# Flamingo cross-attention with experts on one core: the first two pairs' key/value work moved ahead of x's transposes

## The chip, the cores and the metric

The kernel runs on one core of a Trainium2 chip. The metric is the time of one execution in device microseconds (us). Engines are named as in the profile: PE is TensorE (PEld its weight loads), DVE is VectorE, ACT is ScalarE, POOL is GpSimd, SP is SyncE, which here only issues DMAs. A trailing q (SPq, ACTq) marks an engine's sequencer, which issues transfers.

## The reference, cut to what matters

There are 16 batches of 56 rows of x with 256 features, and for each batch 1500 context rows with 256 features. A mask marks padding at the end of each batch's context.

```python
x = x + tanh(g_xattn) * xattn(layernorm(x), ctx, mask, Wq, bq, Wk, bk, Wv, bv, Wo, bo, gamma, beta, rs)
x = x + tanh(g_ffn) * ffn(layernorm(x), router_gate, gate_up, down)   # 8 experts, top 2
...
q = clean(hs @ Wq.T + bq); k = clean(at @ Wk.T + bk); v = clean(at @ Wv.T + bv)   # 16 heads of 16
scores = clip(where(mask > 0.5, clip(q @ k.T / 4, -50, 50), -10000), -50, 50)
probs = softmax(scores); ctx = probs @ v
delta = layernorm(clip(rs, 0, 0.3) * (ctx @ Wo.T + bo)) * gamma + beta
```

A masked position gets a score of -50, not nothing, so every context row counts in the sums. The kernel adds those with plain sums over the whole context and does keys, values and scores only for tiles of 125 context rows that have a key to attend to.

## The kernel before, in words

**Tiles and pairs.** The context is cut into 12 tiles of 125 rows per batch. Two tiles are worked together as a pair: `k_proj` (L538) makes the pair's keys in one PSUM bank, ACT copies them out with the bias `bk` (`k_copy`, L893), `v_proj` (L545) makes the values in another bank, DVE copies them out with the bias `bv` (`v_copy`, L1134), `scores` (L555) multiplies keys by queries, ACT takes the exponentials (`exps`, L901), DVE clips them (`clips`, L1143), `p_v` (L566) multiplies by the values, and DVE adds the result to `acc` (L1156). `first_kv(n)` is `k_proj` and `v_proj` for pair n of the first four. There is one key bank and one value bank, so a key product waits for ACT's copy of the one before, and a value product for DVE's.

**Two stretches.** The last tile of every batch is in every case worked ("sure" tiles). The first four pairs (flow `first`, batches 0 to 7) are sure tiles and need no list; they fill the time in which x is normalised, the queries are made, and the mask is turned into a list of active tiles (`ranks`, L707 and L708; `lists`, L717 to L724). The list then steers the main pairs: a part of them stands in branches on the number of tiles (`early_pairs`), the rest follows in a row. After them come the experts: 32 steps with `gate_up` (L808) and `down` (L823).

**x's way.** x arrives in two halves (SP, L254 and L257). For each, DVE takes the statistics (L1092, L1098), POOL gives a first guess of the inverse root (L382), DVE refines it (`offsets`, up to L1104), ACT normalises eight tiles of 112 rows (`normalise_rows`, L920), DVE cleans each of them in two steps (`clean_rows`, L1111 and L1112), PE transposes them two at a time (`x_transposes(c)`, L523), ACT copies the transposed rows out (`x_rows`, L865), PE makes queries (`x_queries`, L530), ACT adds `bq` (`query_bias`, L877), DVE cleans them in six steps (`clean_queries`, L1123 to L1129), and ACT spreads them by head (`spread_queries`, L886). `x_transposes(c)` waits for the cleaned tiles 2c and 2c + 1.

**The order** on each engine is written out by hand. Each engine runs its own list, waits on semaphores, and never passes a waiting instruction. SP's queue and ACT's queue issue the transfers in the order of the code. Where the stretch with the first pairs ends, SP fetches the whole context of batch after batch in transfers of 1.5 MB (`fetch_all`, L284) for the plain sums (ACT L913, DVE L1173); each such buffer is fetched again only after its sums are taken.

Of the kernel before, what the change touches and what calls it, by code (L numbers as in the profile page):

```python
# [15 lines left out]
P = 128  # L16
# [11 lines left out]
RPH = PAIRS // 2  # L28
# [41 lines left out]
def flamingo(nc, x_d, ctx_d, mask_d, gx_d, gf_d, wq_d, bq_d, wk_d, bk_d, wv_d, bv_d, bv_col_d, wo_d, bo_d,  # L70
             gamma_d, beta_d, rs_d, router_d, gate_up_d, down_d, out_d):
    with ExitStack() as ctx:
# [94 lines left out]
        x_in = [sem(f"x_in{h}") for h in range(2)]  # L167
        bias_in, small_in, late_in, experts_in = (sem(n) for n in ("bias_in", "small_in", "late_in", "experts_in"))
        pair_in = [sem(f"pair_in{n}") for n in range(RING)]
        all_in = [sem(f"all_in{n}") for n in range(STREAMS)]  # L170
# [75 lines left out]
        def _(sp):  # L246
# [3 lines left out]
            def fetch_sure(n, tile, semaphore):  # L250
                for t in range(2):
                    sp.dma_start(tile[:, t], sure_rows[2 * n + t, :, NT - 1]).then_inc(semaphore, 16)

            sp.dma_start(x_sb[:, 0:RPH], x_rows[:, 0:RPH]).then_inc(x_in[0], 16)  # L254
            fetch_sure(0, ctx_pair[0], first_in[0])
            sp.dma_start(mask_i[:], mask_d.rearrange("(h n) t -> n h t", h=2)).then_inc(mask_in, 16)
            sp.dma_start(x_sb[:, RPH:PAIRS], x_rows[:, RPH:PAIRS]).then_inc(x_in[1], 16)  # L257
            for n in range(1, SURE):
                fetch_sure(n, ctx_pair[n], first_in[n])
# [259 lines left out]
        def _(pe):  # L519
# [76 lines left out]
            def first_kv(n):  # L596
                pe.wait_ge(first_in[n], 32)
                after(pe, first.k_out, n)
                k_proj(ctx_pair[n], first.k_mm)
                if n == 0:  # L600
                    ranks()
                    pe.wait_ge(wv_in, 16)
                after(pe, first.v_out, n)
                v_proj(ctx_pair[n], first.v_mm)
# [136 lines left out]

            pe.wait_ge(wk_in, 16)
            first_kv(0)
            pe.wait_ge(consts, CONSTS_IDENT)
            x_transposes(0)
# [4 lines left out]
            lists()  # L750
            first_kv(1)
            first_scores(0)
# [110 lines left out]
        def _(act_e):  # L863
# [84 lines left out]

            act_e.dma_start(wk[:], wk_d).then_inc(wk_in, 16)
            act_e.dma_start(wv[:], wv_d).then_inc(wv_in, 16)  # L950
            act_e.dma_start(wq[:], wq_d).then_inc(wq_in, 16)
            for tile, source in ((bq, bq_d), (bk, bk_d), (bv_col, bv_col_d)):
                act_e.dma_start(tile[:], source).then_inc(bias_in, 16)
            act_e.dma_start(bv[:], bv_d.partition_broadcast(P)).then_inc(bias_in, 16)
            act_e.wait_ge(spare_clear, 1)
# [5 lines left out]
            def first_exps(n):  # L961
                act_e.wait_ge(mask_ready, 1)
                exps(first, p[n % 2], sure_slots(n), n + 1)

            act_e.wait_ge(x_offset, 1)
            for t in range(RPH):
                normalise_rows(t, x_normal)
            act_e.wait_ge(bias_in, 64)
            first_copy(0)
            x_rows(0)  # L970
            x_rows(1)
            query_bias(0)
            act_e.wait_ge(x_offset, 2)
# [6 lines left out]
            spread_queries(0)  # L980
            first_copy(1)
            first_exps(0)
# [78 lines left out]
        def _(dve):  # L1061
# [281 lines left out]
            moments_of(range(RPH, PAIRS))  # L1343
            for t in range(RPH):
                clean_rows(t)
# [16 lines left out]
                                    ALU.add).then_inc(head_ready, 1)  # L1362
            dve.wait_ge(bias_in, 64)
            v_copy(first, v[0], 1)
            clean_queries(0)
# [8 lines left out]
            clean_queries(1)  # L1374
            v_copy(first, v[1], 2)
            clean_rows(4)
# [12 lines left out]
            first_sums(1)  # L1389
            clean_queries(3)  # L1390
            clips(first, p[1], 7)
            first_sums(2)
            dve.wait_ge(small_in, 48)
# [159 lines left out]
```

## Time and profile before

| what | value |
|---|---|
| median of 3 runs | 266.04 us (265.19 to 266.28) |
| the profiled execution's own time | 265.4 us |
| its span, first to last instruction | 263.7 us |
| PE busy | 226.5 us, 86% of the span |
| DVE busy | 180.2 us, 68% |
| ACT busy | 146.3 us, 55% |
| mean granted TensorE clock | 0.939 of full speed |

Times in the rows below are counted from the span's start. The chain is the work that ended last, followed back from the last instruction; "issue" in it is time in which the engine waited for nothing that the profile shows. A granted clock of 1.00 is 2.4 GHz, 0.50 is 1.2 GHz; in the stretch before the first record of the clock the view repeats that first record's value.

### The profile page before, as it was taken

The page shows a single profiled execution, that of the slowest core. Times are in us where ns is not written, and L with a number is a line of the kernel's source. Part 1 is how long each engine was busy: PE and PEld are TensorE (multiplying, and loading weights), DVE is VectorE, ACT ScalarE, POOL GpSimd, SP SyncE. Part 2 cuts the span into 40 slices and gives each one's busy share as a digit, 9 for nine tenths or more (in the row PEclk, how much of TensorE's full clock was granted, in tenths as well). Part 3 has the DMA queues.
Part 4 walks back from the last instruction along what each step waited for, and adds up shares of the span by engine and source line. Part 5 has one row for each costly group of instructions (what it writes and reads, how often), then busy time and mean ns, then how long its engine had stood idle before and what let it go on. Part 6 is the DMA issues. An engine that isn't in the chain of part 4 may idle for free.

```text
span 263.7 us, 7332 instructions
## 1 busy us (share of the span) xinstructions
PE 226.5 (86%) x2820; PEld 195.4 (74%) x2820; DVE 180.2 (68%) x458; ACT 146.3 (55%) x242; POOL 55.8 (21%) x90
## 2 busy tenths in 40 slices
PE   0889897218999999999999979968999489999994
PEld 0777786206888888988888868956899379899993
DVE  1888639710555899865968878687298866865754
ACT  2855679931445779879858781434453136525110
POOL 2470000200143442110002201164114523300000
PEclk9999999556999999999999988999899959999998
DMA  6999304580682289996997000120010000100101
GB/s 218 308 424 413 116 9 114 171 344 2 209 348 60 65 317 340 365 409 191 320 420 301 2 4 2 28 48 0 0 37 1 0 0 2 35 1 0 39 0 35
DMA packets 12871, 37.58 MB, mean 143 GB/s; under 512 B 2320, under 2 KB 10016, under 8 KB 10528
## 3 DMA queue, kind: packets, MB, share of 16 engines
q1 hardware_dynamic: 11728, 36.13, 38.4%
q10 hardware_dynamic: 1008, 0.92, 1.4%
q8 instruction: 25, 0.41, 0.6%
q14 instruction: 14, 0.11, 0.2%
q0 software_dynamic: 96, 0.00, 0.0%
HBM read 35.14 MB, written 0.92 MB: 137 GB/s over the span
## 4 chain that ended last, share of the span: by engine, by line
PE 59%; DVE 17%; issue 12%; ACT 4%; DMA 3%; POOL 3%; SPq 1%; DVEq 0%; ACTq 0%; POOLq 0%
PE bank L808 12%; PE bank L538 11%; PE bank L545 10%; PE bank L566 6%; PE bank L823 6%; PE bank L555 6%; DMA x_sb<-x_dram 3%; POOL guess L382 2%; PE bank L530 2%; PE bank L700 1%; PE bank L523 1%; DVE half_var L1084 1%; DVE stats L1092 1%; DVE acc L1156 1%; DVE normed L1112 1%
## 5 line engine op out<-in xcount | busy, mean ns | idle before, releaser
L808 PE MATMUL bank<-rowsT,gate_up 128*128 128x224 f32 x256 | 58.7, 377 | 0.0
L538 PE MATMUL bank<-ctx_pair,wk 128*128 128x250 f32 x152 | 40.7, 411 | 17.3 <-issue 9.8
L901 ACT ACTIVATE p<-bank,mask_bias,mask_scale 125x896 f32<-125x896 f32 x38 | 39.7, 1095 | 26.7 <-PE bank L555 26.7
L808 PEld LDWEIGHTS bank<-rowsT,gate_up 128*128 128x128 f32 x256 | 51.4, 204 | 2.5 <-issue 0.3
L538 PEld LDWEIGHTS bank<-ctx_pair,wk 128*128 128x128 f32 x152 | 29.2, 202 | 22.9 <-issue 18.0
L545 PE MATMUL bank<-wv,ctx_pair 128*125 128x256 f32 x152 | 37.1, 388 | 0.0
L1021 ACT ACTIVATE silu<-bank 128x224 f32<-128x224 f32 x32 | 11.4, 357 | 46.2 <-PE bank L808 46.2
L1143 DVE TENSOR_SCALAR p<-p 125x912 f32<-125x912 f32 x38 | 27.5, 739 | 11.1 <-ACT p L901 11.1
L823 PE MATMUL bank<-down,act 128*112 128x256 f32 x128 | 33.5, 388 | 0.3 <-DVE act L1443 0.3
L545 PEld LDWEIGHTS bank<-wv,ctx_pair 128*125 128x125 f32 x152 | 29.4, 194 | 4.6
L913 ACT ACTIVATE ctx_all<-ctx_all 128x1500 f32<-128x1500 f32 x19 | 27.9, 1474 | 0.0
L453 POOL COPY q_slot<-qbd 128x224 f32 x22 | 10.9, 496 | 78.6 <-PE bank L555 44.3
L823 PEld LDWEIGHTS bank<-down,act 128*112 128x112 f32 x128 | 23.2, 182 | 4.0 <-DVE act L1443 0.7
L566 PEld LDWEIGHTS bank<-p,v 125*17 125x17 f32 x1344 | 18.2, 99 | 9.1 <-issue 8.4
L382 POOL TENSOR_TENSOR guess<-var_eps,minus_half 112x2 f32<-112x2 f32 (+1 forms) x10 | 9.4, 940 | 72.3 <-DVE var_eps L1077 72.3
L566 PE MATMUL bank<-p,v 125*17 125x57 f32 x1344 | 21.7, 218 | 3.5 <-DVE acc L1156 3.5
L515 POOL TENSOR_TENSOR x_sb<-x_sb,p 112x512 f32<-112x512 f32 x16 | 20.6, 1287 | 18.5 <-ACT p L1029 17.9
L1443 DVE TENSOR_TENSOR act<-silu,bank 128x224 f32<-128x224 f32 x32 | 12.3, 383 | 17.8 <-ACT silu L1021 17.7
L1134 DVE TENSOR_TENSOR v<-bank,bv 125x512 f32<-125x512 f32 x19 | 13.0, 684 | 16.6 <-PE bank L545 16.5
L1156 DVE TENSOR_TENSOR acc<-bank,acc 128x228 f32 (+1 forms) x42 | 16.1, 392 | 9.7 <-DVE acc L1156 4.8
L1029 ACT ACTIVATE p<-bank,weight 112x256 f32<-112x256 f32 x32 | 13.4, 470 | 7.8 <-PE bank L823 5.9
L523 PE MATMUL bank<-ident,normed 112*128 112x112 f32 x32 | 5.1, 285 | 11.1 <-ACT normed L920 7.5
(158 smaller groups left out, 298.4 us busy)
## 6 DMA issues: line engine op xcount, KB each, us to landing
ctx_all<-ctx_dram SPq DMA_DIRECT2D x13, 1500.0 KB, 8.0
ctx_pair<-ctx_dram SPq DMA_DIRECT2D x38, 125.0 KB, 5.2
gate_up<-ctx_dram SPq DMA_DIRECT2D x3, 1500.0 KB, 11.0
gate_up<-gate_up_dram SPq DMA_DIRECT2D x1, 2048.0 KB, 12.8
down<-down_dram SPq DMA_DIRECT2D x1, 1024.0 KB, 14.8
num<-acc SPq DMA_DIRECT2D x16, 57.0 KB
x_sb<-x_dram SPq DMA_DIRECT2D x2, 448.0 KB, 6.1
out_dram<-x_sb SPq DMA_DIRECT2D x4, 224.0 KB, 2.3
```

Of the source, the lines that this page charges most:

```text
L382: nc.gpsimd.tensor_tensor(guess[:, 0:w], var_eps[:, 0:w], minus_half[:, 0:w], ALU.pow).then_inc(guess_out, 1)
L515: nc.gpsimd.tensor_tensor(x_sb[:, rows], x_sb[:, rows], scaled[:, s % 3], ALU.add).then_inc(d_added, 1)
L538: mm = nc.tensor.matmul(bank[:, K_BANK, 2 * TT * m:2 * TT * (m + 1)], wk[:, k, P * m:P * (m + 1)], tile[:, :, k, :], start=(k == 0), stop= ...
L545: mm = nc.tensor.matmul(bank[0:TT, V_BANK, H * t:H * (t + 1)], tile[:, t, k, :], wv[:, k, :], start=(k == 0), stop=(k == HALVES - 1))
L555: mm = nc.tensor.matmul(bank[0:TT, j, DEN * t + R2 * m:DEN * t + R2 * (m + 1)], k_tile[rows, m, TT * t:TT * (t + 1)], q_tiles[t][rows, m]. ...
L566: mm = nc.tensor.matmul(bank[2 * HD * j:2 * HD * j + HD + 1, PV_BANK, ACC * t + SP1 * slot:ACC * t + SP1 * (slot + 1)], v_tile[:, t, v_of( ...
L808: mm = nc.tensor.matmul(bank[:, GU_BANK[s], CHUNK * g:CHUNK * (g + 1)], gate_up[:, e, k, g, :], rowsT[:, k, CHUNK * c:CHUNK * (c + 1)], st ...
L823: mm = nc.tensor.matmul(bank[0:R2, D_BANK[s % 3], H * t:H * (t + 1)], act[:, s % 4, R2 * t:R2 * (t + 1)], down[:, e, :], start=True, stop= ...
L901: nc.scalar.activation(p_tile[:, t].rearrange("t (j n) s -> t j n s", j=4)[:, :, :, 0:S], bank[0:TT, 0:4, DEN * t:DEN * (t + 1)].rearrange ...
L913: nc.scalar.activation(mine, mine, ACT.Identity, accum_out=total[:, k, b:b + 1]).then_inc(act_sum, 1)
L1143: nc.vector.tensor_scalar(tile, tile, E_HI, E_LO, ALU.min, ALU.max).then_inc(flow.p_out, 1)
L1156: nc.vector.tensor_tensor(mine, bank[:, PV_BANK, ACC * t:ACC * (t + 1)].rearrange("p (r s) -> p r s", r=SLOTS), mine, ALU.add).then_inc(fl ...
```

## The change

SP fetches the two tiles of pair 0 ahead of x's first half, and those of pair 1 ahead of the mask and x's second half. ACT's queue fetches `bk` right behind `wk`, with a semaphore of its own, then `wv`, `bv`, `bq`, `bv_col`, and `wq` last instead of third. PE takes keys and values of pair 0, `ranks`, and keys and values of pair 1, and only then x's transposes; before, `ranks` stood inside pair 0 and pair 1 behind `lists`. ACT copies pair 0's keys ahead of normalising x's first half and pair 1's right behind it. DVE copies pair 0's values between the first and the second cleaned tile of x, and pair 1's where pair 0's stood; behind the second `clean_queries` none is left. At the end of the first pairs DVE adds pair 2's sums before it clips pair 3's exponentials, not behind it.

```diff
--- before.py
+++ after.py
@@ -166,6 +166,7 @@
         mask_in, wq_in, wk_in, wv_in = (sem(n) for n in ("mask_in", "wq_in", "wk_in", "wv_in"))
         x_in = [sem(f"x_in{h}") for h in range(2)]
         bias_in, small_in, late_in, experts_in = (sem(n) for n in ("bias_in", "small_in", "late_in", "experts_in"))
+        bk_in = sem("bk_in")
         pair_in = [sem(f"pair_in{n}") for n in range(RING)]
         all_in = [sem(f"all_in{n}") for n in range(STREAMS)]
         pair_in_g = sem("pair_in_g")
@@ -251,11 +252,12 @@
                 for t in range(2):
                     sp.dma_start(tile[:, t], sure_rows[2 * n + t, :, NT - 1]).then_inc(semaphore, 16)
 
+            fetch_sure(0, ctx_pair[0], first_in[0])
             sp.dma_start(x_sb[:, 0:RPH], x_rows[:, 0:RPH]).then_inc(x_in[0], 16)
-            fetch_sure(0, ctx_pair[0], first_in[0])
+            fetch_sure(1, ctx_pair[1], first_in[1])
             sp.dma_start(mask_i[:], mask_d.rearrange("(h n) t -> n h t", h=2)).then_inc(mask_in, 16)
             sp.dma_start(x_sb[:, RPH:PAIRS], x_rows[:, RPH:PAIRS]).then_inc(x_in[1], 16)
-            for n in range(1, SURE):
+            for n in range(2, SURE):
                 fetch_sure(n, ctx_pair[n], first_in[n])
             ctx_rows = ctx_d.rearrange("b p (n f) -> (b p n) f", n=NT)
 
@@ -598,7 +600,6 @@
                 after(pe, first.k_out, n)
                 k_proj(ctx_pair[n], first.k_mm)
                 if n == 0:
-                    ranks()
                     pe.wait_ge(wv_in, 16)
                 after(pe, first.v_out, n)
                 v_proj(ctx_pair[n], first.v_mm)
@@ -741,6 +742,8 @@
 
             pe.wait_ge(wk_in, 16)
             first_kv(0)
+            ranks()
+            first_kv(1)
             pe.wait_ge(consts, CONSTS_IDENT)
             x_transposes(0)
             x_transposes(1)
@@ -748,7 +751,6 @@
             x_queries(0)
             x_queries(1)
             lists()
-            first_kv(1)
             first_scores(0)
             x_transposes(2)
             first_kv(2)
@@ -947,11 +949,12 @@
                                misc(0, 2 * CHUNK).rearrange("p (k n) -> p k n", k=HALVES)).then_inc(misc_out, 1)
 
             act_e.dma_start(wk[:], wk_d).then_inc(wk_in, 16)
+            act_e.dma_start(bk[:], bk_d).then_inc(bk_in, 16)
             act_e.dma_start(wv[:], wv_d).then_inc(wv_in, 16)
+            act_e.dma_start(bv[:], bv_d.partition_broadcast(P)).then_inc(bias_in, 16)
+            for tile, source in ((bq, bq_d), (bv_col, bv_col_d)):
+                act_e.dma_start(tile[:], source).then_inc(bias_in, 16)
             act_e.dma_start(wq[:], wq_d).then_inc(wq_in, 16)
-            for tile, source in ((bq, bq_d), (bk, bk_d), (bv_col, bv_col_d)):
-                act_e.dma_start(tile[:], source).then_inc(bias_in, 16)
-            act_e.dma_start(bv[:], bv_d.partition_broadcast(P)).then_inc(bias_in, 16)
             act_e.wait_ge(spare_clear, 1)
             flat = acc[:].rearrange("p r b s -> p (r b s)")
             nc.scalar.copy(flat, spare[:, 1:2].broadcast_to(flat.shape)).then_inc(zeros_out, 1)
@@ -962,13 +965,15 @@
                 act_e.wait_ge(mask_ready, 1)
                 exps(first, p[n % 2], sure_slots(n), n + 1)
 
+            act_e.wait_ge(bk_in, 16)
+            first_copy(0)
             act_e.wait_ge(x_offset, 1)
             for t in range(RPH):
                 normalise_rows(t, x_normal)
-            act_e.wait_ge(bias_in, 64)
-            first_copy(0)
+            first_copy(1)
             x_rows(0)
             x_rows(1)
+            act_e.wait_ge(bias_in, 48)
             query_bias(0)
             act_e.wait_ge(x_offset, 2)
             for t in range(RPH, RPH + 2):
@@ -978,7 +983,6 @@
                 normalise_rows(t, x_normal)
             act_e.wait_ge(head_ready, 1)
             spread_queries(0)
-            first_copy(1)
             first_exps(0)
             spread_queries(1)
             x_rows(2)
@@ -1341,7 +1345,10 @@
             dve.wait_ge(x_in[1], 16)
             stats_of(range(RPH, PAIRS))
             moments_of(range(RPH, PAIRS))
-            for t in range(RPH):
+            clean_rows(0)
+            dve.wait_ge(bias_in, 48)
+            v_copy(first, v[0], 1)
+            for t in range(1, RPH):
                 clean_rows(t)
             dve.wait_ge(misc_mm, USE["rank"] + 1)
             nc.vector.tensor_copy(rank[:], misc(0, 4, HT)).then_inc(misc_out, 1)
@@ -1360,8 +1367,7 @@
             dve.wait_ge(consts, CONSTS_HEADS)
             nc.vector.tensor_reduce(head_mask[:], head_of[:].rearrange("p (j a) -> p a j", a=2), AX_X,
                                     ALU.add).then_inc(head_ready, 1)
-            dve.wait_ge(bias_in, 64)
-            v_copy(first, v[0], 1)
+            v_copy(first, v[1], 2)
             clean_queries(0)
             dve.wait_ge(misc_mm, USE["list"] + 1)
             nc.vector.tensor_copy(slot_list[:].rearrange("o n s -> o (n s)"), misc(0, 2 * TILES, 1)
@@ -1372,7 +1378,6 @@
             step(nc.vector.tensor_scalar(mask_bias[0:TT], flat_mask, 1.0, CLIP, ALU.subtract, ALU.mult))
             nc.vector.memset(bank[:, PV_BANK, :], 0.0).then_inc(mask_ready, 1)
             clean_queries(1)
-            v_copy(first, v[1], 2)
             clean_rows(4)
             clean_rows(5)
             dve.wait_ge(fill_out, 2 + VRING)
@@ -1388,8 +1393,8 @@
             clips(first, p[0], 5)
             first_sums(1)
             clean_queries(3)
+            first_sums(2)
             clips(first, p[1], 7)
-            first_sums(2)
             dve.wait_ge(small_in, 48)
             step(nc.vector.tensor_scalar(rscale[:], gates[:, 2:3], 0.0, 0.3, ALU.max, ALU.min))
             nc.vector.tensor_scalar(lim[:, 0:1], rscale[0:R2], LIM, None, ALU.mult)
```

PE's list from its first matmul to the third transposes. L538 and L545 are a pair's keys and values, L707 and L708 `ranks`, L523 transposes, L530 queries, L717 to L724 `lists`, L555 scores. Before:

```order
L538 MATMUL bank<-ctx_pair,wk 128x250 x4
L707 MATMUL bank<-active,tri 96x2
L708 MATMUL bank<-active,ones 96x2
L545 MATMUL bank<-wv,ctx_pair 125x256 x4
L523 MATMUL bank<-ident,normed 128x112 x8
L530 MATMUL bank<-rowsT,wq 128x224 x8
L717 MATMUL bank<-pick,vals 1x176 x4
L721 MATMUL bank<-last,attend 125x8 x2
L724 MATMUL bank<-pick,attend 125x176 x2
L538 MATMUL bank<-ctx_pair,wk 128x250 x4
L545 MATMUL bank<-wv,ctx_pair 125x256 x4
L555 MATMUL bank<-qbd,k_sb 125x112 x16
```

The same stretch with the change (its lines stand one or two further on):

```order
L540 MATMUL bank<-ctx_pair,wk 128x250 x4
L547 MATMUL bank<-wv,ctx_pair 125x256 x4
L708 MATMUL bank<-active,tri 96x2
L709 MATMUL bank<-active,ones 96x2
L540 MATMUL bank<-ctx_pair,wk 128x250 x4
L547 MATMUL bank<-wv,ctx_pair 125x256 x4
L525 MATMUL bank<-ident,normed 128x112 x8
L532 MATMUL bank<-rowsT,wq 128x224 x8
L718 MATMUL bank<-pick,vals 1x176 x4
L722 MATMUL bank<-last,attend 125x8 x2
L725 MATMUL bank<-pick,attend 125x176 x2
L557 MATMUL bank<-qbd,k_sb 125x112 x16
```

Pair 1's keys and values went from behind the lists to ahead of the transposes; behind the lists only the scores of pair 0 are left, and then the third transposes.

DVE's list from the variances of x's second half to the copy of `rank`, with the change; before, the same rows stood there without the one of L1138, which is the copy of pair 0's values:

```order
L1115 TENSOR_SCALAR positive<-normed 112x256
L1116 SCALAR_TENSOR_TENSOR normed<-normed,positive 112x256
L1138 TENSOR_TENSOR v<-bank,bv 125x32x16
L1115 TENSOR_SCALAR positive<-normed 112x256
L1116 SCALAR_TENSOR_TENSOR normed<-normed,positive 112x256
```

The copy entered between the first and the second of the four cleaned tiles that the first transposes need.

DVE's list from the clearing of the bank behind the mask's factors to the fifth cleaned tile, before:

```order
L1373 MEMSET bank 128x512
L1123 TENSOR_SCALAR q_clean<-q_raw 128x448
L1124 TENSOR_SCALAR fix_neg<-q_raw 128x448
L1125 TENSOR_SCALAR finite<-q_raw 128x448
L1127 TENSOR_TENSOR q_clean<-q_clean,fix_neg 128x448
L1073 COPY spare<-spare 128x1
L1129 COPY_PREDICATED q_clean<-finite,q_raw 128x448
L1134 TENSOR_TENSOR v<-bank,bv 125x32x16
L1111 TENSOR_SCALAR positive<-normed 112x256
L1112 SCALAR_TENSOR_TENSOR normed<-normed,positive 112x256
```

With the change the same rows stand there but the one of L1134: the copy of pair 1's values left this place.

## Rows read from the trace of the kernel before

**Rows 1.** Chain that ended last: start us, us, what; first transposes to third.

```profile
2.76 7.21 DMA x_sb<-x_dram
...
15.35 0.60 PE bank L523 x4
...
25.01 0.57 issue
...
27.24 0.60 PE bank L523 x4
```

**Rows 2.** Chain that ended last, from the fourth pair to the main pairs.

```profile
46.34 1.06 DVE p L1143 x2
47.40 0.62 DVE acc L1156 x2
...
48.26 1.72 PE bank L566 x64
49.98 7.55 issue
...
58.29 2.26 issue
```

**Rows 3.** Timeline, first 10 us: start, us, engine line op xcount, [idle before <-releaser].

```profile
0.85 0.39 SPq L254 DMA_DIRECT2D x_sb<-x_dram  x1
...
1.29 0.95 SPq L252 DMA_DIRECT2D ctx_pair<-ctx_dram  x2
...
5.76 1.41 DVE L1092 BATCH_NORM_STATS2 stats<-x_sb 112x6 f32<-112x256 f32 x4 [4.38 <-DMA x_sb<-x_dram]
...
7.47 3.67 PE L538 MATMUL bank<-ctx_pair,wk 128*128 128x250 f32 x8 [7.47 <-DMA ctx_pair<-ctx_dram]
...
9.72 0.16 DVE L1104 SCALAR_TENSOR_TENSOR offset<-moments,rstd 112x4 f32<-112x4 f32 x1
```

**Rows 4.** DMA queues, 5 to 6 us: packets, MB, share (q1 SP's, q10 ACT's).

```profile
q10 hardware_dynamic: 136, 0.25, 75.3%
q1 hardware_dynamic: 113, 0.10, 31.2%
```

**Rows 5.** Timeline, 17 to 26 us.

```profile
17.42 0.67 DVE L1134 TENSOR_TENSOR v<-bank,bv 125x512 f32<-125x512 f32 x1
...
20.67 0.84 PE L724 MATMUL bank<-pick,attend 96*125 96x176 f32 x4
20.82 1.23 ACT L886 ACTIVATE qbd<-q_clean,head_mask 128x448 f32<-128x448 f32 x2
...
21.35 1.86 PE L538 MATMUL bank<-ctx_pair,wk 128*128 128x250 f32 x8
...
23.05 1.89 PE L545 MATMUL bank<-wv,ctx_pair 128*125 128x256 f32 x8
...
24.87 1.14 PE L555 MATMUL bank<-qbd,k_sb 32*125 32x112 f32 x32
```

**Rows 6.** Windows: stretch, us, busy of PE, PEld, DVE, ACT, POOL; clock, DMA share, GB/s.

```profile
45.10:47.10 2.00, 0.00 (x0) 0.00 (x0) 1.97 (x5) 1.62 (x3) 0.00 (x0) 1.00 0.46 126
48.20:50.00 1.80, 1.72 (x64) 1.51 (x64) 0.19 (x3) 1.80 (x3) 0.37 (x1) 0.50 0.13 41
60.50:64.20 3.70, 3.65 (x9) 2.97 (x9) 0.00 (x0) 0.54 (x2) 0.00 (x0) 0.50 0.02 4
64.30:66.00 1.70, 1.70 (x35) 1.25 (x37) 0.25 (x1) 0.19 (x1) 0.00 (x0) 1.00 0.00 0
211.70:214.70 3.00, 3.00 (x10) 2.82 (x11) 2.77 (x8) 1.35 (x4) 0.00 (x0) 0.50 0.00 0
214.70:217.80 3.10, 3.10 (x11) 2.50 (x10) 1.76 (x8) 0.72 (x2) 1.94 (x2) 0.50 0.00 0
```

**Rows 7.** Timeline at 49 us: SP's first 1.5 MB fetch behind the first pairs.

```profile
49.23 0.34 SPq L284 DMA_DIRECT2D ctx_all<-ctx_dram  x1
```

**Rows 8.** DMA queues, 54 to 58 us: packets, MB, share of 16 engines.

```profile
q8 instruction: 1, 0.02, 1.4%
```

## The prediction, made before the run

> **What bounds the kernel now.** I read the page first, then the chain of waits, which shows where the start of the kernel is decided; then the timeline of the first 50 us, the windows for the granted clock, and the DMA queues. Up to 60 us the chain is not one engine's: it runs x's transfer, DVE's statistics and cleaning, PE's transposes, queries and lists, DVE's query cleaning, DVE's cleaning of the fifth and sixth tile of x, PE's third transposes [rows 1]. From 27.24 us on PE is packed until the scores of pair 2. Behind the first pairs the chain goes through DVE's clips and sums, PE's last product, and two stretches of 7.55 and 2.26 us in which PE waits for nothing that the profile shows [rows 2]. After that the main pairs run on PE back to back, so what the start loses or gains is passed on to the end.
>
> So the change must be judged by when two things start: the second transposes (15.35 us) and the third (27.24 us) [rows 1]. Both wait for DVE, not for PE.
>
> **The change part by part.**
>
> *Transfers.* x's first half is issued first now, and DVE begins on it at 5.76 us; pair 0's tiles come behind it and release PE at 7.47 us [rows 3]. The change swaps the two. Together they are the same bytes, so x's first half should land at the latest when the tiles did: at most 7.47 - 5.76 = +1.7 us. At least it is issued later by the two issues ahead of it, +0.95 us [rows 3]. Between 5 and 6 us ACT's queue took 75.3% and SP's 31.2% of the DMA engines [rows 4], and with `wq` now last on ACT's queue SP's share there grows a little. I take +1.3. The offsets end at 9.72 + 0.16 = 9.88 us [rows 3] and DVE went on with x's second half at 9.97 (2.76 + 7.21, [rows 1]), so 0.1 of slack is used up: **+1.2 us** (0.8 to 1.7). The second half also has pair 1's tiles ahead of it, again 250 KB, and moves by about as much; DVE reaches it only when the offsets are done, so this isn't added.
>
> The row on the two queues shows them served together. The Trainium skill ("DMA: Bandwidth & Descriptors", section "Queues, rings and completion order") says that each DMA engine takes turns between the queues that have work, and takes one queue's descriptors in order. By that rule x can't pass the tiles on SP's queue, and the delay would be near the upper end; the trace agrees on the sharing, and no row shows the order being broken.
>
> *PE's keys and values ahead of the transposes.* Pair 0 starts with the tiles' landing, before 7.47 us. Its keys took 3.67 us, twice the 1.86 us of pair 1's [rows 3, 5], since TensorE was still at its low clock. Keys and values of both pairs and the ranks fit before the transposes, which DVE releases at about 17 us; only pair 1's values wait, for DVE's copy of pair 0's. I cost this at nothing; the cover is DVE's cleaning, and if PE is still cold at pair 1's values they take 1.7 us more and some 0.9 would show.
>
> *ACT's copies of keys.* Pair 0's now stands ahead of the normalising of x's first half, so all of x waits behind it if the keys or `bk` are late. Even with the old start the keys are done at 7.47 + 3.67 = 11.1 us [rows 3], and the offsets now come at 9.88 + 1.3 = 11.2: nothing, and at most a fraction of a us if the tiles don't land earlier. Pair 1's copy falls where ACT waits for the first transposes: nothing.
>
> *DVE's copy of pair 0's values* now stands between cleaned tiles 1 and 2: 0.67 us [rows 5], on the chain: **+0.7 us**. Before it lay at 17.42 us where DVE waited for the queries; pair 1's copy now has that place and costs nothing there. The second transposes start at about 15.35 + 1.9 = 17.25 us, and queries, lists and the mask's factors shift by as much.
>
> *DVE's copy of pair 1's values* leaves the place behind the second `clean_queries`, where the chain has it as 0.57 us of "issue" at 25.01 [rows 1]: **-0.6 us**. So the third transposes start at 27.24 + 1.2 + 0.7 - 0.6 = 28.5 us.
>
> *The place that pair 1 left on PE.* Before, 1.86 and 1.89 us of keys and values stood between the lists (end 21.51) and the scores of pair 0 at 24.87 [rows 5]. They were not on the chain: DVE's 5.7 us from the lists to the third transposes were. Taking them away brings the scores to the end of the spread queries, 20.82 + 1.23 + 1.9 = 23.95 us, and gains nothing for the third transposes. PE then has 1.14 us of scores in the 5.1 us from 23.4 to 28.5, with the last 3.4 us, from 25.1, idle.
>
> What such a gap does to the clock the trace shows once: PE did its last product of pair 2 by 45.0 us, had nothing to do until 48.26, and the granted clock, still 1.00 (2.4 GHz) to 47.10, was 0.50 (1.2 GHz) when it came back [rows 2, 6]. The low clock then stays for a time after work is back: 3.7 us from 60.50 until it was 1.00 at 64.30, and 6.1 us from 211.70 to 217.80 [rows 6]. Work there takes twice as long, so half of the stretch is lost: 1.85 to 3.05 us. Behind the third transposes PE is packed with keys, values, scores and queries of the chain, so the loss is all on it. The restart is like the one at 60.50 (keys and values without a break), so I take a value near the lower end: **+2.2 us**.
>
> The Trainium skill ("TensorE: Matmul & The Clock Gate", section "Why this matters for your kernels") asks for no long idle gaps between bursts of matmuls, because TensorE falls back to its cold clock. It speaks against this change, and by it the gap costs what I have put in; without it the sum would be that of the first rival. The trace agrees at 48.26 us.
>
> *Sums before clips.* Before: two clips 1.06, sums 0.62, then the product of pair 3, 1.72 [rows 2]. The product needs the sums and for its first half one clip; its second half needs the second clip. With the order turned its first half starts 0.5 us earlier, and it ends 0.5 us earlier. But behind it PE waits 7.55 us, and that stretch ends when code packets come through among the transfers that SP issued at 49.23 [rows 2, 7, 8]. Those hang on ACT's sums, which this edit doesn't move. Between -0.5 and 0, I take **-0.3 us**.
>
> **Sum:** 1.2 + 0.7 - 0.6 + 2.2 - 0.3 = +3.2 us. On the profiled execution (265.4 us) that gives 268.6; it lies 0.6 below the median shown, so against 266.04 the forecast is **269.2 us**. With the bounds of x's delay (0.8 to 1.7), the clock (1.85 to 3.05) and the last edit it runs from +2.3 to +4.9, less if x's delay is overrated.
>
> **The rivals.**
>
> *The clock doesn't fall.* The gap of 3.4 us is about as long as the one that let it fall (3.26), and the scores stand just before it as pair 2's product did there. Against: nothing else in the rows. If it doesn't, or rises at once, the sum is +1.0: 267.0 us. Within half a per cent.
>
> *Faster: code arrives before the transfers.* Of PE's two waits at the branches the first took 7.55 us and the second 2.26 [rows 2]. Between 54 and 58 us a single instruction packet came [rows 8], in a stretch full of the 1.5 MB fetches. The last edit brings PE 0.5 us ahead of ACT's sums, and so of SP's issue at 49.23 [rows 7]. If PE's request then gets ahead of them, the first wait becomes like the second: -5.3 us, the sum 3.2 - 5.3 = -2.1, **263.9 us**. It decides from the point where PE asks before the fetch is in the queues; PE reached the wait at 49.98, 0.75 behind the issue, and 0.5 is short of that. I hold it unlikely but not excluded.
>
> *x isn't late.* If the DMA engines make room for both and x lands as before, the sum is +2.0: 268.0 us. The 0.95 us of issues ahead of it speak against it.
>
> **How the numbers follow.** The forecast has 0.65, the steady clock 0.17, early code 0.13, x on time 0.05. The range of 8 in 10 reaches from 266.4 to 271.4: it takes in the forecast's bounds and the steady clock, and leaves out early code (0.13) and some 0.07 above. A measurement of this kernel can tell about 0.5%, or 1.3 us, from no change: faster 0.13, within 0.5% 0.17 (the steady clock), slower 0.70 (forecast and x on time).
>
> **What would show it.** In the changed profile: DVE's first statistics start near 7 us instead of 5.76, PE's first keys before 7.47; the second transposes near 17.2; an idle gap of more than 3 us ahead of the third transposes, near 28.5; a granted clock of 0.50 behind it, and keys of pair 2 at 3 us or more; the long wait at the branches still there, later by about 3 us. I am wrong if the third transposes start before 27.5 us, if the clock is 1.00 through the gap, or if the wait behind pair 3 shrinks to a few us.

## The result, and the profile after

| | before | changed |
|---|---|---|
| median | 265.62 us (4 runs, 263.01 to 266.28) | 270.68 us (4 runs, 270.14 to 270.99) |
| profiled execution | 265.4 us | 270.92 us |
| its span | 263.7 us | 269.2 us |

The ratio is 1.0207, 95% interval 1.0135 to 1.028: about 5 us slower. The forecast was 269.2 us (range 266.4 to 271.4), slower with 0.70. Ratios, here and below, leave disturbed runs out, so they can lie off the quotient of two medians (e10's rests on three of its ten runs, and the profiled executions of e7 and e10 are disturbed ones). The kernel before was run again beside the experiments; its medians there are 265.4 to 265.7 us, and what is said below to be faster or slower is counted from them.

Chain of waits of the changed kernel (start us, us, what), answering to [rows 1, 2]:

```profile
3.77 9.32 DMA x_sb<-x_dram
...
16.45 2.66 PE bank L547 x8
19.11 1.49 PE bank L525 x8
...
31.63 1.01 PE bank L525 x4
32.64 2.78 PE bank L540 x8
...
52.80 0.55 DVE p L1147
...
53.49 1.05 PE bank L568 x64
54.54 9.25 issue
...
64.54 1.65 issue
66.19 2.92 PE bank L540 x7
```

Three things are new in it. x's second half lands 9.32 us after its issue (7.21 before), at 13.09 instead of 9.97. PE's values of pair 1 (L547 at 16.45) stand on the chain. Keys of pair 2 take 2.78 us, where in the chain of the kernel before they took 1.71.

Timeline of the changed kernel (start, us, engine line op, [idle before <-releaser]), answering to [rows 3, 5]:

```profile
4.93 3.67 PE L540 MATMUL bank<-ctx_pair,wk 128*128 128x250 f32 x8 [4.93 <-DMA ctx_pair<-ctx_dram]
...
7.74 1.40 DVE L1096 BATCH_NORM_STATS2 stats<-x_sb 112x6 f32<-112x256 f32 x4 [6.35 <-DMA x_sb<-x_dram]
...
11.00 0.29 DVE L1340 TENSOR_SCALAR attend<-mask_i 96x250 f32<-96x250 int32 x1 [1.12 <-DMA mask_i<-mask_dram]
...
12.47 1.94 PE L540 MATMUL bank<-ctx_pair,wk 128*128 128x250 f32 x8
...
13.12 1.40 DVE L1096 BATCH_NORM_STATS2 stats<-x_sb 112x6 f32<-112x256 f32 x4 [0.40 <-DMA x_sb<-x_dram]
...
15.71 0.68 DVE L1138 TENSOR_TENSOR v<-bank,bv 125x512 f32<-125x512 f32 x1
...
16.45 2.66 PE L547 MATMUL bank<-wv,ctx_pair 128*125 128x256 f32 x8 [2.04 <-DVE v L1138]
```

Pair 0 starts at 4.93 instead of 7.47 us, so PE does get its tiles early. DVE pays: it waits for x's first half to 7.74 (5.76 before), for the mask to 11.00, and for the second half to 13.12. The mask matters for PE too, since the ranks hang on it. Pair 1's values wait for DVE's copy at 15.71.

Windows of the changed kernel (stretch, us, busy of PE, PEld, DVE, ACT, POOL, then clock, DMA share, GB/s), answering to [rows 6]:

```profile
17.70:21.00 3.30, 3.30 (x13) 2.63 (x12) 3.02 (x15) 0.89 (x2) 2.85 (x7) 0.50 0.99 418
28.50:31.50 3.00, 0.00 (x0) 0.00 (x0) 2.79 (x9) 2.96 (x4) 0.00 (x0) 0.96 0.14 46
31.60:34.60 3.00, 2.97 (x10) 2.56 (x11) 2.42 (x6) 0.67 (x2) 0.00 (x0) 0.50 0.62 156
34.80:37.00 2.20, 2.20 (x11) 1.70 (x10) 0.00 (x0) 0.83 (x2) 0.00 (x0) 1.00 0.00 0
```

The idle gap ahead of the third transposes is there, and the clock is 0.50 behind it. A second low stretch, from 17.70, I had only as a side remark.

### The profile page after: what moved, and what is told of

Its sections match the earlier page's. It is cut to its first block, busy times and chain, and to the rows that moved or that the text cites. A ratio compares the mean times of both kernels' runs of the same rounds, so it can differ in the third digit from the quotient of the medians.

```text
span 269.2 us, 7333 instructions
## 1 busy us (share of the span) xinstructions
PE 229.4 (85%) x2820; PEld 196.4 (73%) x2820; DVE 180.8 (67%) x458; ACT 146.4 (54%) x242; POOL 56.0 (21%) x90
## 4 chain that ended last, share of the span: by engine, by line
PE 60%; DVE 15%; issue 11%; ACT 5%; DMA 3%; POOL 3%; SPq 1%; DVEq 0%; ACTq 0%; POOLq 0%
PE bank L810 12%; PE bank L540 12%; PE bank L547 11%; PE bank L825 7%; PE bank L568 6%; PE bank L557 6%; DMA x_sb<-x_dram 3%; PE bank L525 2%; PE bank L532 2%; POOL guess L384 2%; PE bank L701 1%; DVE half_var L1088 1%; DVE stats L1096 1%; ACT p L1033 1%; PE bank L677 1%
## 5 line engine op out<-in xcount | busy, mean ns | idle before, releaser
L810 PE MATMUL bank<-rowsT,gate_up 128*128 128x224 f32 x256 | 57.9, 373 | 0.0
L540 PE MATMUL bank<-ctx_pair,wk 128*128 128x250 f32 x152 | 41.7, 419 | 15.8 <-issue 10.9
L810 PEld LDWEIGHTS bank<-rowsT,gate_up 128*128 128x128 f32 x256 | 50.3, 200 | 2.3 <-issue 0.3
L540 PEld LDWEIGHTS bank<-ctx_pair,wk 128*128 128x128 f32 x152 | 30.1, 209 | 21.6 <-issue 11.6
L547 PE MATMUL bank<-wv,ctx_pair 128*125 128x256 f32 x152 | 37.8, 394 | 2.0 <-DVE v L1138 2.0
L825 PE MATMUL bank<-down,act 128*112 128x256 f32 x128 | 34.9, 400 | 0.6 <-DVE act L1448 0.6
L547 PEld LDWEIGHTS bank<-wv,ctx_pair 128*125 128x125 f32 x152 | 29.7, 196 | 7.2 <-DVE v L1138 2.4
L1147 DVE TENSOR_SCALAR p<-p 125x912 f32<-125x912 f32 x38 | 27.4, 738 | 10.7 <-ACT p L903 10.7
L825 PEld LDWEIGHTS bank<-down,act 128*112 128x112 f32 x128 | 24.1, 189 | 4.6 <-DVE act L1448 0.9
L1138 DVE TENSOR_TENSOR v<-bank,bv 125x512 f32<-125x512 f32 x19 | 13.0, 684 | 19.2 <-PE bank L547 19.2
L568 PEld LDWEIGHTS bank<-p,v 125*17 125x17 f32 x1344 | 17.6, 97 | 8.5 <-issue 7.8
L568 PE MATMUL bank<-p,v 125*17 125x57 f32 x1344 | 21.0, 213 | 2.9 <-DVE p L1147 2.6
```

The lines of the kernel that those rows point to most:

```text
L540: mm = nc.tensor.matmul(bank[:, K_BANK, 2 * TT * m:2 * TT * (m + 1)], wk[:, k, P * m:P * (m + 1)], tile[:, :, k, :], start=(k == 0), stop= ...
L547: mm = nc.tensor.matmul(bank[0:TT, V_BANK, H * t:H * (t + 1)], tile[:, t, k, :], wv[:, k, :], start=(k == 0), stop=(k == HALVES - 1))
L568: mm = nc.tensor.matmul(bank[2 * HD * j:2 * HD * j + HD + 1, PV_BANK, ACC * t + SP1 * slot:ACC * t + SP1 * (slot + 1)], v_tile[:, t, v_of( ...
L810: mm = nc.tensor.matmul(bank[:, GU_BANK[s], CHUNK * g:CHUNK * (g + 1)], gate_up[:, e, k, g, :], rowsT[:, k, CHUNK * c:CHUNK * (c + 1)], st ...
L825: mm = nc.tensor.matmul(bank[0:R2, D_BANK[s % 3], H * t:H * (t + 1)], act[:, s % 4, R2 * t:R2 * (t + 1)], down[:, e, :], start=True, stop= ...
L1147: nc.vector.tensor_scalar(tile, tile, E_HI, E_LO, ALU.min, ALU.max).then_inc(flow.p_out, 1)
```

## The experiments

To compare them, this table gives for each profiled execution the start of x's second statistics, of the first query products, of the third transposes, of pair 1's scores, and of PE's first transposes behind the main pairs ("behind"), then its span, and last the median of the label's runs. All are starts in the timelines, in us.

| run | statistics | queries | third | scores 1 | behind | span | median |
|---|---|---|---|---|---|---|---|
| before | 10.00 | 15.79 | 27.24 | 31.21 | 153.91 | 263.7 | 265.62 |
| changed | 13.12 | 20.57 | 31.63 | 37.08 | 159.03 | 269.2 | 270.68 |
| e1 | 11.23 | 17.65 | 28.48 | 35.25 | 157.88 | 265.3 | 266.64 |
| e2 | 12.80 | 18.95 | 31.93 | 35.90 | 158.93 | 267.8 | 270.05 |
| e3 | 11.93 | 17.82 | 30.86 | 34.82 | 157.98 | 266.9 | 267.42 |
| e4 | 13.77 | 21.66 | 32.50 | 36.47 | 160.60 | 269.4 | 271.60 |
| e5 | 10.27 | 18.55 | 29.38 | 35.03 | 157.34 | 267.5 | 269.46 |
| e6 | 13.84 | 19.61 | 32.07 | 38.46 | 161.02 | 268.0 | 269.76 |
| e7 | 10.11 | 15.89 | 27.34 | 31.31 | 152.26 | 262.2 | 263.21 |
| e8 | 10.08 | 15.88 | 27.32 | 31.29 | 154.31 | 263.2 | 265.44 |
| e9 | 12.13 | 18.55 | 29.38 | 36.39 | 159.18 | 268.0 | 268.95 |
| e10 | 14.30 | 20.08 | 30.85 | 34.82 | 157.78 | 270.9 | 269.72 |
| e11 | 10.16 | 15.96 | 26.73 | 30.70 | 153.54 | 260.4 | 262.93 |
| e12 | 10.41 | 16.20 | 26.97 | 30.94 | 150.81 | 258.0 | 260.80 |

The stretch from "behind" to the end is the same program on PE in all of them, and yet, with e10 left out, it takes from 106.9 us (e11) to 110.2 us (the changed kernel). The clock does that, as the last section shows. So I judge the moves by the columns up to "behind", and the medians only beside them.

**e1: the old order on SP.** The changed kernel with

```diff
-            fetch_sure(0, ctx_pair[0], first_in[0])
             sp.dma_start(x_sb[:, 0:RPH], x_rows[:, 0:RPH]).then_inc(x_in[0], 16)
-            fetch_sure(1, ctx_pair[1], first_in[1])
+            fetch_sure(0, ctx_pair[0], first_in[0])
...
-            for n in range(2, SURE):
+            for n in range(1, SURE):
```

> The changed kernel with SP's old order of transfers (x's first half first, pair 1 behind x's second half), all else as changed. Theory (x's transfers are the largest part, 3.1 us of the delay of DVE's second statistics at 13.12 against 10.00): DVE's second statistics start near 10.2 us, the time falls from 270.7 to 267.5 to 268.5; PE's own work ahead of the transposes (pair 0 starts only at 7.5 again) may become what ends last there. Rival (the order on PE and DVE costs it, the transfers hardly): 270 us or more.

Measured: 266.64 us (ratio to before 1.006, interval 1.0008 to 1.0113). The statistics start at 11.23, not at 10.2, so SP's order is not all of x's lateness. The median is below my range, but it must not be read as the price of the transfers: "behind" is only 1.2 us earlier than in the changed kernel, and 2.8 us of the profiled execution's gain came after it, with the clock. Pair 1's scores and "behind" are still 4 us later than before: 1.2 us of that stood at the third transposes, and 2.8 came behind them, where the clock was low again (27.4 to 34.2 us).

**e2: SP's new order alone.** The kernel before with the reverse of that edit.

> The kernel before with SP's new order of transfers alone. Theory: x's second half lands 1.5 to 3 us later and all of it reaches the end, 267.2 to 268.7. Rival (ACT's queue order makes x late, SP's order hardly): under 266.5. Nothing on PE changes order, so the clock should stay up ahead of the third transposes.

Measured: 270.05 us (1.0193, 1.0126 to 1.026), above my range and as slow as the whole change. Ahead of the third transposes the clock was up, as I had expected, but it had been low before:

```profile
11.90:16.00 4.10, 3.73 (x11) 3.12 (x12) 3.75 (x19) 2.78 (x6) 2.26 (x9) 0.50 1.07 411
16.00:22.00 6.00, 5.31 (x19) 4.22 (x18) 4.46 (x17) 1.06 (x2) 4.92 (x13) 0.50 1.01 416
```

These are windows of e2. Pair 0's keys were done at 8.8 us; then PE waited for the ranks, so for the mask (its row starts at 11.13), and its values and both query products ran at 1.2 GHz: the query products took 4.73 us instead of 3.21. So a late mask can cost through the clock as well: from the second statistics to the third transposes it took 19.13 us, before 17.24.

**e3: ACT's new queue order alone.** The kernel before with `wq` last:

```diff
+            act_e.dma_start(bk[:], bk_d).then_inc(bias_in, 16)
             act_e.dma_start(wv[:], wv_d).then_inc(wv_in, 16)
+            act_e.dma_start(bv[:], bv_d.partition_broadcast(P)).then_inc(bias_in, 16)
+            for tile, source in ((bq, bq_d), (bv_col, bv_col_d)):
+                act_e.dma_start(tile[:], source).then_inc(bias_in, 16)
             act_e.dma_start(wq[:], wq_d).then_inc(wq_in, 16)
-            for tile, source in ((bq, bq_d), (bk, bk_d), (bv_col, bv_col_d)):
-                act_e.dma_start(tile[:], source).then_inc(bias_in, 16)
-            act_e.dma_start(bv[:], bv_d.partition_broadcast(P)).then_inc(bias_in, 16)
```

> The kernel before with ACT's new queue order alone (bk, wv, bv, bq, bv_col, then wq last). Theory of the prediction (moving wq back gives SP's queue more): x's second half lands no later than 9.97 and the time is 265.6 or a little less. Rival (the small and the late transfers of ACT's queue now run against x's second half, which took 9.32 us from its issue instead of 7.21): second half 1 us or more later, 266.5 to 267.5.

Measured: 267.42 us (1.0052, 1.0018 to 1.0087). The rival holds. From e3's timeline:

```profile
9.64 0.29 DVE L1337 TENSOR_SCALAR attend<-mask_i 96x250 f32<-96x250 int32 x1 [1.87 <-DMA mask_i<-mask_dram]
...
11.93 0.43 DVE L1093 BATCH_NORM_STATS2 stats<-x_sb 112x6 f32<-112x256 f32 x1 [0.57 <-DMA x_sb<-x_dram]
```

The mask is 1.5 us and x's second half 1.9 us later, with SP's list untouched. Putting `wq` last did not give SP's queue room where it was needed. Here too the clock adds to it: it was 0.50 from 17.7 to 21.1 us, behind two idle stretches of PE ahead of the transposes (2.54 and 1.09 us), and the query products took 4.79 us. So ACT's order alone has the third transposes 3.6 us late and "behind" 4.1.

**e4: the gap filled.** The changed kernel with

```diff
             first_scores(0)
+            pe.wait_ge(first.k_out, 2)
+            for _ in range(2):
+                queries(bank[:, K_BANK], 0)
             x_transposes(2)
```

> The changed kernel with 8 more matmuls (pair 0's query product twice over, written to the idle key bank, result unused) between the scores of pair 0 and the third transposes, where PE idles 3.2 us. Theory (that gap drops TensorE's clock): granted clock 1.00 behind the third transposes, keys of pair 2 in 1.9 us instead of 2.99, 1.0 to 1.8 us faster, 269 to 269.7. Rival (the low clock there is hidden or has another cause): 270.5 or slower.

Measured: 271.6 us (1.0221, 1.0125 to 1.0317), so no faster. But the mechanism is as the theory has it. Windows of e4:

```profile
29.20:32.40 3.20, 3.20 (x20) 2.95 (x16) 2.99 (x10) 3.00 (x4) 0.00 (x0) 1.00 0.16 38
32.50:34.60 2.10, 2.10 (x13) 1.93 (x13) 1.95 (x5) 0.62 (x2) 0.00 (x0) 1.00 0.84 201
```

From the third transposes to pair 1's scores it takes 3.97 us (before 3.97, changed 5.45): the low clock behind the gap costs 1.48 us, and work in the gap takes it away. In this run part of the gain was eaten before: statistics 0.65 us later, queries 1.09 later than in the changed kernel. 0.6 us of it was still there at pair 1's scores (36.47 against 37.08) and at the end of the last product of the first pairs (53.92 against 54.54). The wait at the branches swallowed it: the next keys start at 65.94 without a break (changed 63.78 for the first product and 66.19 for the rest) and take 3.67 us, and the clock stayed low to 71.2 us (68.8 in the changed kernel).

**e5: both old queues, the new order on the engines.** The changed kernel with the edit of e1, and ACT's queue as before (the reverse of e3's edit).

> The changed kernel's order on PE, DVE and ACT, but both queues of transfers as before. Separates the moves on the engines from the transfers. Theory (transfers cost some 4 us, the moves on the engines together about 1): 265.5 to 267; second statistics at 10.0 as before, third transposes near 27.3 to 28.5, an idle gap of 3 us ahead of them and a low granted clock behind it. Rival (without the late x the moves gain, since PE has less to do between lists and scores): 264.5 or less.

Measured: 269.46 us (1.0164, 1.0108 to 1.0221). Neither case: even with x on time the moves cost. From e5's timeline:

```profile
13.77 0.69 DVE L1136 TENSOR_TENSOR v<-bank,bv 125x512 f32<-125x512 f32 x1 [0.32 <-PE bank L546]
...
15.57 1.89 PE L546 MATMUL bank<-wv,ctx_pair 128*125 128x256 f32 x8
17.29 0.93 PE L524 MATMUL bank<-ident,normed 112*128 112x112 f32 x8
```

With pair 0 starting at 7.6 us, PE has four products ahead of the transposes and reaches them only at 17.29; DVE's cleaned tiles no longer cover it. The third transposes are 2.1 us late, and behind the idle gap ahead of them (3.21 us) the clock was low from 29.5 to 33.0 us, for another 1.7. "Behind" is +3.4 us, SP's order alone (e2) +5.0, the whole change +5.1. The parts don't add up, since they wait for the same things: tiles early without the new order on PE is no use, and the new order with tiles late is none either.

**e6: pair 0's value copy earlier.** The changed kernel with

```diff
+            dve.wait_ge(bias_in, 48)
+            v_copy(first, v[0], 1)
             dve.wait_ge(x_in[1], 16)
             stats_of(range(RPH, PAIRS))
             moments_of(range(RPH, PAIRS))
-            clean_rows(0)
-            dve.wait_ge(bias_in, 48)
-            v_copy(first, v[0], 1)
-            for t in range(1, RPH):
+            for t in range(RPH):
                 clean_rows(t)
```

> The changed kernel with DVE's copy of pair 0's values moved from behind the first cleaned tile to ahead of the second half's statistics, where DVE waits for x. Theory (0.7 us on DVE's chain and a delay of pair 1's values, which came back at the low clock and held the second transposes 0.9 us): second transposes 0.7 to 1.7 us earlier against the start of the second statistics, time 269 to 270. Rival (the copy is hidden): no difference, 270.7.

Measured: 269.76 us (1.0181, 1.0128 to 1.0234). From statistics to queries it takes 5.77 us (changed 7.45, before 5.79): the copy among the cleaned tiles and the values behind it cost 1.68 us together, at the upper end of what I expected. But little of it is kept: the clock fell at 20.0 us, the query products took 4.89 us (changed 3.49), and from statistics to third transposes it takes 18.23 us against 18.51, so 0.3 less. Statistics started 0.72 later here, and the low clock behind the third transposes lasted to 37.1 us.

**e7: the context fetches held back.** The kernel before with

```diff
             fetch_pair(6)
+            sp.wait_ge(main.k_mm, 4)
             fetch_all(4)
```

> The kernel before with one wait more on SP: the first 1.5 MB fetch behind the first pairs is issued only once PE has finished the keys of the fourth main pair, so after PE's branches. Theory (the first code wait, 7.55 us, lasts until the transfers let a code packet through): that wait falls to 2 to 4 us, the main pairs start 3 to 5 us earlier, 261 to 263. Rival (code arrives at its own pace, transfers or not): the main pairs start at 57.5 to 60.5 as before, and the time is 265.6 or more, since the context arrives later.

Measured: 263.21 us (0.9893, 0.9853 to 0.9933), 2.4 us faster, between my two cases. Timeline of e7 and, behind it, of e8, both PE:

```profile
48.37 1.06 PE L567 MATMUL bank<-p,v 125*17 125x57 f32 x64 [3.26 <-DVE acc L1157]
55.99 0.76 PE L539 MATMUL bank<-ctx_pair,wk 128*128 128x250 f32 x1 [6.56 <-issue]
58.67 1.82 PE L539 MATMUL bank<-ctx_pair,wk 128*128 128x250 f32 x4 [1.92 <-issue]
```

```profile
47.69 1.41 PE L566 MATMUL bank<-p,v 125*17 125x57 f32 x64 [2.60 <-DVE p L1143]
57.66 0.76 PE L538 MATMUL bank<-ctx_pair,wk 128*128 128x250 f32 x1 [8.56 <-issue]
```

Without the transfers the main pairs start 1.6 to 1.9 us earlier, not 3 to 5, and the wait is still 6.56 us. In the DMA view of 52 to 54 us e7 has a 16 KB instruction packet (`q8 instruction: 1`), the kernel before none; its packet came between 54 and 58 [rows 8]. So the transfers are the smaller part of the wait. That the rest is the fetching of code itself fits these packets, but is not shown: the profile names nothing that PE waits for there.

**e8: sums ahead of clips, alone.** The kernel before with `clips(first, p[1], 7)` and `first_sums(2)` exchanged.

> The kernel before with only DVE's sums of pair 2 put ahead of the clips of pair 3. Theory (the code wait ends with the transfers, which this does not move): PE's product of pair 3 ends 0.5 us or more earlier, the wait behind it is longer by as much, 265.3 to 265.9, no difference that can be measured. Rival (the wait has a fixed length): 264.9 to 265.1 or, if PE's request gets ahead of the transfers, 260 to 261.

Measured: 265.44 us (0.9993, 0.995 to 1.0037), no difference. The theory holds to the tenth: the product ends 0.9 us earlier (49.1 against 49.98), the wait is 8.56 instead of 7.55 us, and the next keys start at 57.66 against 57.54.

**e9: only pair 0 ahead of x.** The changed kernel without `fetch_sure(1, ...)` ahead of the mask.

> The changed kernel, but pair 1's tiles go back behind x's second half; pair 0's stay ahead of x. Splits the lateness of x. Theory (250 KB per pair, so each costs its part): the second half's statistics start at 11 to 12 us instead of 13.12, the mask's row at 9 to 10 instead of 11.00, the first transposes behind the main pairs at 157.5 to 158.2 instead of 159.03, time 269 to 270. Rival (pair 0's place alone does it): statistics at 12.8 or later and 270.5.

Measured: 268.95 us (1.0141, 1.0072 to 1.021). Statistics at 12.13 and the mask's row at 10.04: pair 1's place costs 1.0 us of each. The third transposes came 2.3 us earlier than in the changed kernel. "Behind" did not follow (159.18), though: the clock was low from 28.8 to 35.6 us behind them.

**e10: the three suspected causes out.** The changed kernel with the edits of e1, e4 and e6.

> The changed kernel's order of keys and values on PE, with all three suspected causes taken out: x and the mask ahead as before on SP, pair 0's value copy ahead of the second half's statistics, and 8 filling matmuls in PE's gap ahead of the third transposes. Theory (these three are the whole loss): third transposes at 27 to 28 us with the clock at 1.00 behind them, scores of pair 1 near 31 to 32.5, the first transposes behind the main pairs at 153.5 to 155 (before 153.91, changed 159.03), time 264.5 to 266.5. Rival (something else in the moved order costs time): transposes behind the main pairs at 156 or later.

Measured: 269.72 us (264.04 to 272.63; 1.0057, 0.9989 to 1.0126), no difference that can be told from none. My edit undid itself: with x first, pair 0 starts at 7.31 us, DVE's early copy waits for its values to 13.69, and the second statistics behind it start at 14.30 instead of some 11. The clock did stay at 1.00 behind the gap (transposes to scores 3.97 us). Whether the three causes are the whole loss stays open.

**e11: pair 1's value copy later, in the kernel before.**

```diff
-            v_copy(first, v[1], 2)
             clean_rows(4)
             clean_rows(5)
+            v_copy(first, v[1], 2)
```

> The kernel before with DVE's copy of pair 1's values moved behind the fifth and sixth cleaned tile, the one gain that I counted for the change (0.6 us). Theory: third transposes at 26.7 instead of 27.24, 0.6 us kept to the end, 265.0. Rival (the wait moves to pair 2's values or to the clips, or the code wait swallows it): third transposes at 26.7 but main pairs no earlier, 265.6.

Measured: 262.93 us (0.9943, 0.9899 to 0.9987). Third transposes at 26.73 and "behind" at 153.54, 0.5 and 0.4 us earlier; from queries to third transposes it takes 10.77 us instead of 11.45, the whole of the copy. In between, the rival holds: the last product of the first pairs ends 0.5 us earlier (49.46 against 49.98), but the next keys are back at 60.48 instead of 60.55, so the wait at the branches took the gain, and the 0.4 at "behind" comes from values at a higher clock there (2.01 us against 2.29). The median fell by 2.5 us, outside both forecasts. In the profiled execution 2.9 of 3.3 us come behind "behind", with the clock, so little of it is this edit's work.

**e12: a version that beats both.** The kernel before with the edits of e7, e8 and e11.

> The kernel before with three small edits: SP holds its 1.5 MB fetches until PE is past its branches (took 2.4 us off alone), DVE's copy of pair 1's values behind the fifth and sixth cleaned tile, and DVE's sums of pair 2 ahead of the clips of pair 3. Theory: with the transfers out of the way the code wait no longer ends with them, so the two DVE edits now come through: 261.5 to 262.7. Rival (the code packets' own pace ends the wait whatever PE does before): 263.2, as with the held fetch alone.

Measured: 260.8 us (258.76 to 262.33; 0.9853, 0.9793 to 0.9914), below my range, 4.6 us faster than before and 9.9 than the change. Its chain:

```profile
46.07 0.58 DVE acc L1157 x2
46.65 0.55 DVE p L1144
...
47.33 1.72 PE bank L567 x64
49.05 6.07 issue
55.12 0.76 PE bank L539
55.88 1.68 issue
57.56 2.66 PE bank L539 x6
```

PE is back at 57.56 us (before 60.55, e7 58.67) and "behind" at 150.81, 3.1 us earlier than before. So against e7 the DVE edits came with 1.1 us more at the keys. They start PE's last product 1.0 us earlier (47.33 against 48.37), of which 0.7 is lost again, since it ran at the low clock (1.72 us against 1.06); and the two waits behind it were 0.7 us shorter together (6.07 and 1.68 against 6.56 and 1.92). That the edits shortened them isn't shown. What the three edits do together is shown only as a whole.

## Why the prediction was right

Direction, range and the place of the loss held; the size was too small, 3.2 us forecast and 5.1 measured (4.6 against the 266.04 us that the forecast was counted from). That the range held owes something to luck: two terms were 1.9 and 1.0 us too low, the clock behind the gap was 0.7 too high, and 0.8 us of what had been lost by pair 1's scores was made good before PE's first transposes behind the main pairs. Step by step, in the profiled executions:

- **x's lateness**, "+1.2 us (0.8 to 1.7)": measured 13.12 - 10.00 = +3.1. This is the step that failed most. I took it from x's first half, and even that was 2.0 us late, beyond my upper bound. Then I wrote off the second half ("moves by about as much; DVE reaches it only when the offsets are done"). It moved by 3.1 us and DVE waited for it, though only for the last 0.40 us: the offsets, held up by the first half and by the mask's row (1.12 us of waiting), were done at 12.71 instead of 9.88. The bound "the same bytes" left out that pair 1's tiles, and with them the mask, add bytes ahead of the second half (e9: 1.0 us), and that ACT's reordered queue costs 1.9 us by itself (e3), where I had it as a small gain. The mask, which I had not priced, came 2.9 us late.
- **The value copy among the cleaned tiles**, +0.7: the row is 0.68 us. Right.
- **PE's early keys and values**, "nothing", with "some 0.9 would show" if PE was cold: PE was at 1.2 GHz from 17.7 to 21.0 us and the queries start 4.78 us later, 0.98 more than x's lateness and the copy. The price that I named for the exception was met, but the reason was another: PE was not still cold, for pair 1's keys at 12.47 took 1.94 us. It waited 2.04 us for DVE's copy of pair 0's values, which stands behind x's late second half, and the clock fell at 17.7, in the values behind that wait.
- **The value copy taken out**, -0.6: from queries to third transposes 11.06 us against 11.45, so -0.4, with query products 0.3 us longer at the low clock; e11 gives 0.7. About right.
- **The clock behind the gap**, +2.2 (1.85 to 3.05): the gap was 3.22 us, the clock fell, the cost 1.48 us. Right in kind, too high by 0.7, because the low clock ended 3 us behind the transposes, sooner than in either row that I had priced it by. e4 shows it as the gap's doing. The size is a draw: e5, e6, e1 and e9 have the same gap (3.21 to 3.41 us), and from third transposes to pair 1's scores they lose 1.7, 2.4, 2.8 and 3.0 us against the kernel before. So 2.2 was a fair middle and the changed kernel's 1.48 the mildest; what decides it no run here shows.
- **Sums before clips**, -0.3: nothing (e8). The reason given for "between -0.5 and 0" was the right one, and 0 should have been taken.

In all 3.1 + 0.7 + 1.0 - 0.4 + 1.5 = +5.9 at pair 1's scores (37.08 against 31.21). Behind that the last product of the first pairs ends only 4.6 us later (54.54 against 49.98), and the wait at the branches, from there to the second row of keys, is 1.1 us longer (11.65 against 10.57), so it swallows that gain as it did e8's. It is +5.6 at the main pairs' keys (66.19 against 60.55), +5.1 behind them, and +5.5 at the end.

Of the rivals, "the clock doesn't fall" and "x isn't late" are refuted by the rows above. "Code arrives before the transfers" had a true core with a wrong price: the transfers hold the wait up by 1.6 to 1.9 us (e7), not by 5.3. I had priced it by the other, shorter wait at the branches, and the two are not alike. The rule of the Trainium skill ("TensorE: Matmul & The Clock Gate", section "Why this matters for your kernels") on idle gaps pointed the right way: the trace and e4 agree, with 1.48 us for a gap of 3.22.

## What to carry to other kernels

An engine that is idle early is not worth feeding at the price of the transfer that the chain hangs on: here PE started 2.5 us sooner and the chain 3.1 us later. When transfers are reordered, price each one that stands behind the moved ones, on both queues, by its own landing, and also those that look small (the mask). Work taken out from between two waits of TensorE is not free even where it was not on the chain; it had kept the clock up, and the gap that it left cost 1.5 to 3.0 us in the five kernels that have it.

## What the runs showed of the hardware that I had not expected

**The clock in the last part shifts the total by microseconds.** From "behind" to the end the same PE instructions took 106.9 to 110.2 us. The granted clock was at 0.50 for some 7 us of that stretch in e11, for some 14 us in the kernel before (109.8 us) and in the changed one (110.2 us). One place: the first expert products behind the main pairs, in e1 (first row) and in e5 (second row):

```profile
160.20:163.40 3.20, 3.20 (x21) 2.92 (x25) 2.83 (x9) 2.61 (x4) 0.00 (x0) 1.00 0.00 0
```

```profile
159.90:164.50 4.60, 4.60 (x20) 4.07 (x21) 3.31 (x10) 2.46 (x4) 0.00 (x0) 0.70 0.00 0
```

The 16 rows of L809 took 3.27 us in the one and 4.65 in the other. In the first the granted clock stayed at 2.4 GHz; in the second it fell at 159.3 us, in the small router products just ahead, and was back at 162.7. So two kernels whose starts differ by 0.5 us can end 2 us apart (e1 265.3, e5 267.5, with "behind" at 157.88 and 157.34), the wrong way round. A median difference of 1 to 2 us in this kernel says little on the edit alone; the start of a row behind the edited stretch says more.

**The transfers at the start lose speed with their order.** Between 6 and 8 us the DMA view shows 318 GB/s before and 188 GB/s in the changed kernel:

```profile
DMA packets 529, 0.38 MB, mean 188 GB/s; under 512 B 162, under 2 KB 529, under 8 KB 529
```

It is the line of the changed kernel. Before, there were 1009 packets in those 2 us. ACT's order makes the difference: with ACT's queue as before it is 314 GB/s (e5) and 272 GB/s (e2, SP's new order), with ACT's new order alone 199 GB/s (e3). Which of ACT's moved transfers does it (`bv`'s broadcast, the small biases or `wq`) was not tried.
